# Attention over 722 context rows: one tile of 122 rows and five of 120, instead of five of 128 and one of 82

## The reference, cut to what matters

```python
# x (32, 100, 512), ctx_1024 (32, 722, 512); 16 heads of 32
def xattn(q, k, v, wq, bq, wk, bk, wv, bv, wo, bo):
    qh = (q @ wq + bq).reshape(b, -1, H, HD).transpose(0, 2, 1, 3)
    kh = (k @ wk + bk).reshape(b, -1, H, HD).transpose(0, 2, 1, 3)
    vh = (v @ wv + bv).reshape(b, -1, H, HD).transpose(0, 2, 1, 3)
    scores = softmax(einsum('bhqd,bhkd->bhqk', qh, kh), axis=-1)
    attn = einsum('bhqk,bhkd->bhqd', scores, vh)
    ...
    return concat @ wo + bo
x = x + tanh(g_xattn[0]) * xattn(layernorm(x), ctx_1024, ctx_1024, ...)
x = x + tanh(g_ffn[0]) * masked_self_attention(layernorm(x), ...)
```

## Time and profile before

| | us |
|---|---|
| median of 3 runs | 2627.3 (2623.84 to 2627.86) |
| the profiled execution | 2630.54 |
| its span, first to last instruction | 2628.7 |
| PE busy | 2528.6 (96%) |
| weight loads busy | 2294.1 (87%) |
| VectorE busy | 1804.5 (69%) |
| ScalarE busy | 1332.8 (51%) |
| GpSimd busy | 383.6 (15%) |
| score matmuls (L844), 3072 | 531.4 |
| mix matmuls (L859), 3072 | 556.4 |

### The profile page before, as it was taken

One profiled execution on the slowest core, in us unless ns is written; L12 is line 12 of the kernel. 1 busy time (PEld: TensorE's weight loads), 2 busy tenths in 40 slices (PEclk: granted clock), 3 DMA queues, 4 the chain that ended last, 5 costly groups with the idle time before them and its releaser, 6 DMA issues. The chain is left out here.

```text
span 2628.7 us, 47776 instructions
## 1 busy us (share of the span) xinstructions
PE 2528.6 (96%) x17376; PEld 2294.1 (87%) x17376; DVE 1804.5 (69%) x2869; ACT 1332.8 (51%) x3000; POOL 383.6 (15%) x281
## 2 busy tenths in 40 slices
PE   7899999999999999999999999999969999599999
PEld 6889999999999999999999999999858888588887
DVE  7467777777777777777777777777657666354665
ACT  3345555555555545554555555555434444354554
POOL 0311111111111111111111111111133433000000
PEclk9999999999999999999999999999779999696999
DMA  7645545555455555555544555545379999888892
GB/s 221 204 118 133 128 119 130 128 131 123 127 129 128 130 123 129 123 131 129 128 129 121 130 129 131 129 116 124 88 180 212 209 217 200 163 181 164 181 191 72
DMA packets 324830, 379.91 MB, mean 145 GB/s; under 512 B 126332, under 2 KB 232220, under 8 KB 324636
## 3 DMA queue, kind: packets, MB, share of 16 engines
q1 hardware_dynamic: 322772, 375.80, 60.2%
q10 hardware_dynamic: 1864, 1.43, 0.2%
HBM read 162.57 MB, written 72.57 MB: 89 GB/s over the span
## 5 line engine op out<-in xcount | busy, mean ns | idle before, releaser
L735 DVE TENSOR_TENSOR c_parted<-c_prob,c_parted 128x600 fp32r<-128x600 f32 x512 | 400.6, 783 | 372.0 <-ACT c_prob L681 372.0
L859 PE MATMUL c_mix<-c_parted,c_v 128*66 128x200 f32 (+1 forms) x3072 | 556.4, 271 | 0.7 <-DVE c_parted L735 0.6
L844 PE MATMUL c_pair<-c_q_stack,c_k_stack 100*128 100x100 f32 (+1 forms) x3072 | 531.4, 230 | 3.4 <-DVE c_parted L735 1.6
L844 PEld LDWEIGHTS c_pair<-c_q_stack,c_k_stack 100*128 100x128 f32 (+1 forms) x3072 | 522.1, 187 | 8.8 <-ACT c_prob L681 3.1
L721 DVE TENSOR_REDUCE c_peak<-c_pair 100x1 f32<-100x724 f32 x512 | 456.7, 907 | 56.1 <-PE c_pair L806 40.7
L677 ACT ACTIVATE c_parted<-c_pair 128x600 fp32r<-128x600 f32 x512 | 344.8, 673 | 290.9 <-PE c_pair L844 290.8
L859 PEld LDWEIGHTS c_mix<-c_parted,c_v 128*66 128x66 f32 (+1 forms) x3072 | 421.3, 141 | 2.8 <-DVE c_parted L735 0.9
L681 ACT ACTIVATE c_prob<-c_pair 128x600 f32<-128x600 f32 x512 | 341.6, 667 | 0.0
L659 ACT ACTIVATE c_v<-c_work 128x512 fp32r<-128x512 f32 x192 | 115.7, 603 | 441.5 <-PE c_work L91 441.5
L806 PE MATMUL c_pair<-c_k_stack,c_q_stack 96*100 96x362 f32 x1024 | 254.2, 329 | 0.0
L1652 ACT ACTIVATE s_prob<-s_scores,s_shift 106x100 f32<-106x100 f32 x512 | 170.2, 363 | 146.0 <-DVE s_shift L1685 146.0
(11 more groups left out here) (200 smaller groups left out, 5325.9 us busy)
## 6 DMA issues: line engine op xcount, KB each, us to landing
c_k_stack<-c_k_hi SPq DMA_DIRECT2D x1024, 90.2 KB, 2.1
e_stage<-in_ctx SPq DMA_DIRECT2D x32, 1444.0 KB, 6.4
c_k_stack<-c_k_lo SPq DMA_DIRECT2D x512, 90.2 KB, 2.1
c_q_stack<-q_parts SPq DMA_DIRECT2D x192, 100.0 KB, 2.4
mix_parts<-w_mixed SPq DMA_DIRECT2D x64, 200.0 KB, 3.2
r_parts<-mix_parts SPq DMA_DIRECT2D x22, 512.0 KB, 7.5
s_q_stack<-qk_parts SPq DMA_DIRECT2D x10, 800.0 KB
s_k_stack<-qk_parts SPq DMA_DIRECT2D x10, 800.0 KB
```

What stands on the lines that cost most here:

```text
L735: dve.tensor_tensor(p[:, :, 1, :], prob[i % 2][:], p[:, :, 0, :], ALU.subtract).then_inc(p_lo_done, 1)
L844: return pe.matmul(pair[i % 2][0:r, t // (CT // 2), col:col + S], k_stack[:, i, t * P:t * P + r], q_stack[:, i, :], start=True, stop=True)
L859: return pe.matmul(mix[g % 2][0:VW, at * 2 * S:(at + 1) * 2 * S], v[0:r, t, i, :], parted[i % PR][0:r, t, :, :].rearrange("p a s -> p (a s)"),
```

## The change

The tiles of context rows become even: 722 // 6 // 2 * 2 = 120 rows for tiles 1 to 5, and the remaining 122 for tile 0. `c_cols(t)` gives the columns of a tile, and the value products and the scores use it. The rows to be cleared are now the last 32 partitions over all six tiles' columns, in both banks, since every tile is shorter than 128.

```diff
 CT = -(-C // P)
-C_LAST = C - (CT - 1) * P
+C_EVEN = C // CT // 2 * 2
+C_FIRST = C - (CT - 1) * C_EVEN
...
         def c_rows(t):
-            return P if t < CT - 1 else C_LAST
+            return C_EVEN if t else C_FIRST
+
+        def c_cols(t):
+            at = C_FIRST + (t - 1) * C_EVEN if t else 0
+            return slice(at, at + c_rows(t))
...
             for i in range(2):
-                dve.memset(pair[i][P // 2:P, 1, (CT // 2 - 1) * S:CT // 2 * S], 0.0).then_inc(padded, 1)
+                dve.memset(pair[i][P - HD:P, :, 0:CT // 2 * S], 0.0).then_inc(padded, 1)
...
                         r = c_rows(i)
-                        cols = slice(i * P, i * P + r)
+                        cols = c_cols(i)
...
                 return pe.matmul(pair[i % 2][0:r, t // (CT // 2), col:col + S],
-                                 k_stack[:, i, t * P:t * P + r], q_stack[:, i, :], start=True, stop=True)
+                                 k_stack[:, i, c_cols(t)], q_stack[:, i, :], start=True, stop=True)
```

## The result

The changed kernel takes 2612.5 us (median of 8 runs, 2608.9 to 2619.95). Eight runs of the kernel before, among them the three shown first with their median of 2627.3 us, have a median of 2624.7 us. The ratio is 0.996, with a 95% interval of 0.9941 to 0.9979: faster by 0.4%.

A forecast was written before the change was run, and what follows sets the result against it. PE was taken to bound the batches, through weight loads or matmul streams. Terms -6.7 + 0.3 + 1.0 - 0.6 - 0.25 gave -6.3 us from the 2627.3 us median: 2621.0 us, 0.24% less; range 2617 to 2626.8.

The forecast's parts named there:

- What bounds the kernel: Context stage, 200 to 1850 us: PE alone sets the pace for 30 batches of 55.02 us; full-width score tiles bound by loads.
- The price of 120 columns: Score-tile weight loads: on a line of 0.84 ns a column, 120 columns take 105.3 ns, 6.7 less than 128.
- Rival 1: Score loads: 120 columns cost as much as 128, full width being favoured; 11.4 us lost, 2638.7 us; chance 0.07.
- tile 5 of a mixed step before: Steps scoring one head and mixing another: the 82-column load takes 94 ns, bound by the mix matmul's stream; ends 92 and 100.
- mixed step, the five exposed loads: 434 steps: tiles 1 to 4 save 26.8 ns, tile 5 loses 11.3; net 15.5 ns saved, 6.7 us in all.
- step of scores alone, five loads: Heads 0 and 1, 63 steps at full clock: 522 to 526.5 ns, 4.5 ns lost each, 0.3 us.
- held value load after head 0: First held value part after head 0's scores, load from 82 to 120 columns: 30 ns lost, 32 times, 1.0 us.
- value load after a transpose: Exposed value load after three of the shift's four transposes: 120 instead of 128 columns saves 6.7 ns, 96 times, 0.6 us.
- The last batch: Last batch at half clock, 1.2 GHz: cheaper score loads save 18 ns a head, 14 heads, 0.25 us.
- Rival 3: Last batch: starting 6 us earlier, one or two more heads run at half clock; 2622 to 2623 us; chance 0.18.
- Rival 2: Batches: an engine off PE has nearly the same period and absorbs the gain; 2627.3 us or slightly less; chance 0.12.
- The two clearing instructions: Stage's start, VectorE: from 0.25 us together to 1.5 us, hidden before its next work; 1.3 us once if uncovered.

## Why the prediction was right or wrong

**What bounds the kernel: right.** PE still has no row among the waits from 200 to 1850 us, VectorE still waits for ScalarE (337.8 us) and ScalarE for PE.

**The price of 120 columns: right.** 184 ns shown; averaged over the mixed steps, a load of tiles 2 to 5 takes 105.2 ns up to the start of the next one, against 105.3 from the line (tile 1, behind the hidden load, 106.7). Rival 1 is dead: loads of 118, 120, 122 and 128 columns show 182, 183 to 184, 183 and 188 to 190 ns, so there is no step between 100 and 128 and no fast load at 128. The Trainium skill ("TensorE: Matmul & The Clock Gate", section "Weight-path perf modes") excludes the type FP32 from its fast weight load; the profile shows these operands as f32, and the trace agrees with the exclusion. With its exclusion the rule never spoke for rival 1, other than the prediction begins by saying.

**The terms** (averages of the distances between load starts, all mixed steps, steps of scores alone or transposes from 205 to 1818 us of the two traces):

| | predicted | measured |
|---|---|---|
| tile 5 of a mixed step before | 94 ns (92 to 100) | 94.1 |
| mixed step, the five exposed loads | -15.5 ns | 542.9 to 527.6: -15.3 |
| step of scores alone, five loads | +4.5 ns | 518 to 523: +5 |
| held value load after head 0 | +30 ns | 75.0 to 106.7: +32 |
| value load after a transpose | -6.7 ns | 110.3 to 104.4: -5.9 |
| batch | -198 ns | -173 |
| 31 batches | -6.1 us | -5.3 |

The batch gives 25 ns less than its terms. The distances between load starts, added up by kind over 29 batches (two profiles of the kernel before, three of the changed one), show where: the loads of the mix's value tiles, which the sum put at nothing because their 66 columns don't change, take 25 ns a batch more. Most of it is the one behind the last score tile of each mixed step, 59.1 ns before and 60.4 now, 14 times. Its reason wasn't tested. All else nearly cancels: score loads 216 ns less (208 forecast), value products 12 more (10 forecast), transposes 8 more, keys and peak products within 3.

**The last batch: a small term under a large variation.** I put 0.25 us for its cheaper loads. The loads came as forecast: at half clock a score load takes 218 ns with 128 columns, 205 with 120 and 170 with 82, so 17 ns a head are saved. But where the clock falls inside the batch moves its length between 34.9 and 37.4 us over both kernels, and where it falls alike the two agree within 0.2 us (35.4 and 35.3 us at 0.70, 37.0 and 37.2 at 0.57), so the 0.25 us can't be seen. Rival 3 named this mechanism. Its sign doesn't follow from the earlier start that it gives as the reason: if the fall stood still in time, an earlier batch would have fewer heads at half clock. In the first pair of profiles the clock falls 2.3 us later and the batch starts 6.6 us earlier, and 1.7 us are gained where rival 3 loses 1 to 2.

**The step that failed: the base and the scatter.** "I take differences to the median" of three runs, 2627.3 us, and "1.4 us of scatter" in the low end. The three runs lay 4 us apart, and I took this for the kernel's spread. The low end added only those 1.4 us to the terms of the tiles, so it had no room for half-clock stretches that fall otherwise. Forty-three runs have 2611.6 to 2637.8 us, a standard deviation of 5.8 and a mean of 2622.3: the base was 5 us too high. The page of before had the sign: in its self-attention a slice at 6 tenths of the clock, which comes and goes. The profiled execution, a fourth one beside the three, was one with a long self-attention, 357.0 us where the six profiles of the two kernels have 343.0 to 357.0. With the sum unchanged, 2622.3 - 6.3 = 2616.0 us was the number to give; the 20 runs of the changed kernel have a mean of 2615.3. The gain itself was hit: 6.3 forecast, 6.9 with a standard error of 1.6 measured over all runs. The first comparison alone, 12.2 us between its medians, is twice that. From a scatter of 5.8 us, a median of eight runs scatters by some 2.5 us (an estimate), and the difference of two by some 3.6; no kernel here shows a mechanism of the tiles for the rest. That the forecast gain is so near 6.9 is in part luck: the batches show 5.3 us of it, 0.8 less than their forecast 6.1. What makes the half-clock stretches come in one execution and not in another stays open.

**The other steps.** The two clearing instructions take 1.19 us together, in place of 0.25 (1.5 forecast), and are hidden as forecast: VectorE then waits 3.53 us for its next work.

```profile
111.62 1.19 DVE L702 MEMSET c_pair<- 32x600 f32 x2 [3.19 <-PEq L153]
116.33 0.59 DVE L720 SCALAR_TENSOR_TENSOR c_k_lo<-c_work,f_key_bias,c_k_hi 128x362 fp32r<-128x362 f32 x1 [3.53 <-ACT c_k_hi L674]
```

Tile 0 and the value products behind 512 columns cost nothing that can be seen. Rival 2 didn't come about: the batch shrank to 54.86 us.

## What to carry to other kernels

Where weight loads alternate with short matmuls, cost each load as the larger of its own time and the stream of the matmul beside it, one by one. Its own time is here 5 ns and 0.83 ns a column, from the steps of scores alone: 73.3 ns for 82 columns, 78.3 for 88, 91.7 for 104, 103.4 for 118, 105.0 for 120 and 111.7 for 128. A fixed number of columns is then best divided evenly over the exposed loads, with the surplus in the one that a long matmul hides; a narrow remainder tile is wasted below the stream's floor (96 ns beside 200 columns).

Before you forecast a time, ask what the runs' own spread is: three runs that agree within 0.15% said nothing about a kernel whose runs spread over 1%. Steady repetition within one trace, 55.03 against 54.85 or 54.86 us in every profile, shows a change of 0.2% of the whole that no single pair of runs can.

## What the runs showed of the hardware that I had not expected

The half-clock time of a stage can differ from one execution of the same kernel to the next: the changed kernel's last batch took 35.3 or 37.4 us, its self-attention 343.0 or 354.8 us, at a granted clock of 0.94 or 0.90. The self-attention's two lengths give (2 x 0.10 x 354.8) - (2 x 0.06 x 343.0) = 30 us more at half clock for 11.8 us more time, 0.4 us for each. Whether small shifts of a stage's start move these stretches, as theory P has it, the profiles here leave open.
